# Eight padding copies made one per buffer, and expert blocks placed some steps earlier, in an attention and mixture-of-experts kernel

## The reference

```
qkv  = x @ qkv_w.T                       # q and k are rotated
attn = einsum(q, k) * SCALE + alibi
w    = softmax(attn);  out = w @ v       # per batch and head
x    = layernorm(x + out @ proj_w.T + proj_b)
shared = silu(x @ sW1 + sb1) @ sW2 + sb2
top_vals, top_idx = top_k(sqrt(softplus(x @ routing_W.T + bias)), 2)
y_e  = silu(x @ rW1[e] + rb1[e]) @ rW2[e] + rb2[e]      # e = 0..7
x    = layernorm(x + shared + sum over the two chosen e of top_val * y_e)
```

## Time and profile before

| | |
|---|---|
| median of three runs | 1526.68 us |
| profiled execution, its time | 1523.36 us |
| its span in the trace | 1521.5 us |
| PE busy | 1384.0 us, 91% |
| DVE busy | 1150.9 us, 76% |
| ACT busy | 1019.2 us, 67% |
| POOL busy | 722.4 us, 47% |
| moved by DMA | 242.07 MB, 159 GB/s on average |
| clock granted to TensorE, mean | 0.971 of full |

### The profile page before, as it was taken

How to read it: one execution, slowest core, us unless ns; L and a number is a source line. 1 busy time by engine, 2 the same in 40 slices (tenths; PEclk the granted TensorE clock), 3 DMA queues, 4 the chain that set the end, 5 groups by cost and what they waited for, 6 DMA issues and landing times.

```text
span 1521.5 us, 34124 instructions
## 1 busy us (share of the span) xinstructions
PE 1384.0 (91%) x11166; PEld 751.6 (49%) x11166; DVE 1150.9 (76%) x2632; ACT 1019.2 (67%) x1742; POOL 722.4 (47%) x654
## 2 busy tenths in 40 slices
PE   7889989999999989999999999999899988886777
PEld 4434444444444434555555544454455655445545
DVE  7777878788888887777776778778887777743677
ACT  1367767677777767777777777676677777765434
POOL 1434373645555454644526353625566443545441
PEclk8899999999999999999999999999999999999898
DMA  7434453434444334554656353445568777468542
GB/s 210 143 89 136 143 155 109 139 112 138 120 126 129 105 123 137 174 184 158 196 155 201 115 162 101 151 144 167 175 206 261 232 225 230 121 204 285 177 146 84
DMA packets 172777, 242.07 MB, mean 159 GB/s; under 512 B 58247, under 2 KB 91102, under 8 KB 172350
## 3 DMA queue, kind: packets, MB, share of 16 engines
q1 hardware_dynamic: 142170, 181.18, 39.3%
q0 software_dynamic: 10752, 29.37, 6.0%
q10 hardware_dynamic: 19684, 29.33, 5.5%
HBM read 152.53 MB, written 91.44 MB: 160 GB/s over the span
## 4 chain that ended last, share of the span: by engine, by line
PE 63%; DVE 13%; SPq 7%; issue 6%; DMA 5%; POOL 3%; ACT 3%; another core or an unknown queue 1%; ACTq 0%; POOLq 0%; DVEq 0%
PE pS L674 14%; PE pV L729 13%; PE pG L753 6%; PE pS L682 5%; DVE negm L990 4%; PE pG L762 4%; PE pG L775 3%; PE pG L856 3%; PE pG L864 3%; PE pG L848 2%; PE pG L837 2%; PE pT L706 1%; DMA rb<-d_rec 1%; ACT ee L1438 1%; PE pT L698 1%
## 5 line engine op out<-in xcount | busy, mean ns | idle before, releaser
L990 DVE TENSOR_REDUCE negm<-pS 128x1 f32<-128x512 f32 x1024 | 657.6, 682 | 210.5 <-PE pS L674 175.6
L1438 ACT ACTIVATE ee<-pT,slp 128x512 f32<-128x512 f32 x1024 | 650.9, 685 | 208.0 <-PE pT L698 171.4
L674 PE MATMUL pS<-ka,qa 62*128 62x512 f32 x1024 | 394.9, 453 | 7.4 <-ACT ee L1438 4.5
L698 PE MATMUL pT<-qa,ka 64*128 64x512 f32 x1024 | 393.4, 451 | 0.0
L682 PEld LDWEIGHTS pS<-mAB,tri 64*128 64x128 bf16 x2048 | 117.1, 96 | 424.2 <-issue 398.4
L682 PE MATMUL pS<-mAB,tri 64*128 64x64 bf16 x2048 | 236.9, 196 | 69.7 <-DVE negm L990 35.3
L729 PE MATMUL pV<-ee,vv 128*32 128x512 f32 (+1 forms) x2048 | 283.1, 625 | 0.0
L706 PE MATMUL pT<-mAB,tri 64*128 64x64 bf16 x2048 | 236.2, 196 | 4.5 <-ACT ee L1438 3.9
L1622 POOL TENSOR_TENSOR raw<-raw,rope 128x512 f32<-128x512 f32 x61 | 78.1, 1280 | 257.7 <-DVE sh L1027 257.1
L674 PEld LDWEIGHTS pS<-ka,qa 62*128 62x128 f32 x1024 | 172.6, 191 | 36.3 <-DVE negm L990 22.0
L698 PEld LDWEIGHTS pT<-qa,ka 64*128 64x128 f32 x1024 | 172.3, 190 | 0.0
(11 more groups left out here) (203 smaller groups left out, 2247.6 us busy)
## 6 DMA issues: line engine op xcount, KB each, us to landing
d_part<-parts SPq DMA_DIRECT2D x63, 512.0 KB, 2.8
qa<-d_part SPq DMA_DIRECT2D x378, 64.0 KB
wb<-in_wb SPq DMA_DIRECT2D x77, 256.5 KB
xg<-d_x SPq DMA_DIRECT2D x77, 256.0 KB
d_y<-yb ACTq DMA_DIRECT2D x77, 256.0 KB
ka<-d_part SPq DMA_DIRECT2D x128, 128.0 KB
xT<-in_xT SPq DMA_DIRECT2D x16, 512.0 KB
ka<-d_part SPq DMA_DIRECT2D x128, 64.0 KB
```

Source lines behind the costliest of these rows:

```text
L674: last = e.matmul(pS[:, k, :], qa[g % 4][r, i, t * 128:t * 128 + 128].bitcast(F32R), ka[g % 4][r, i, :].bitcast(F32R), start=(k == 1), sto ...
L698: last = e.matmul(pT[:, k, :], ka[g % 4][r, i, kt * 128:kt * 128 + 128].bitcast(F32R), qa[g % 4][r, i, :].bitcast(F32R), start=(k == 1), s ...
L990: e.tensor_reduce(negm[:, g % 2, j, t + k:t + k + 1], pS[:, k, :], AX, ALU.max, negate=True).then_inc(s_max, 1)
L1438: e.activation(ee[:, k, d % 7, :], pT[:, k, :], ACT.Exp, scale=slp[:, 6, h:h + 1]).then_inc(s_exp, 1)
```

## The change

Three things are changed. The paddings are issued as two DMAs, one for each buffer, at step 43, and each writes the 256 padding rows of all eight regions; before, two DMAs of one region each stood at the steps 43, 51, ... 99. The wait for them is for two DMAs' semaphore counts (32), where it was for sixteen (256). The blocks of the first group stand at 90 + 4j where they stood at 96 + 4j (the first 25 of them), and the first 27 blocks of the second group at 92 + 2j where they stood at 96 + int(1.85j). The later blocks of both groups, the third group and the final steps stay.

```
-BLOCKS_AT = ((96, 4.0, 25, 252, 4.0), (96, 1.85, 27, 148, 2.0), (104, 1.25, 15, 128, 3.0))
+BLOCKS_AT = ((90, 4.0, 25, 252, 4.0), (92, 2.0, 27, 148, 2.0), (104, 1.25, 15, 128, 3.0))
...
-                e.wait_ge(pad_w, 32 * E)
+                e.wait_ge(pad_w, 32)
...
-            if 0 <= s - PADS < 8 * E and (s - PADS) % 8 == 0:
-                r0 = (s - PADS) // 8 * REGION
+            if s == PADS:
                 for i in range(2):
-                    e.dma_start(d_x[i][r0:r0 + ROWS], A["x"][0, 0:ROWS]).then_inc(pad_w, 16)
+                    e.dma_start(d_x[i].rearrange("(x r) c -> r x c", x=E)[0:ROWS],
+                                A["x"][0, 0:ROWS].rearrange("r (x c) -> r x c", x=1).broadcast_to([ROWS, E, C])
+                                ).then_inc(pad_w, 16)
```

## The result

The changed kernel is slower: a median of 1540.94 us (1537.17 to 1551.62, six timed runs) against 1526.34 us for the kernel before on the same chip, a ratio of 1.0115 with a 95% interval of 1.0087 to 1.0143, that is +17.6 us (13 to 22). The two medians themselves differ by 14.6 us, and the median of all 25 runs of the changed kernel on record is 1543.1; I go by the ratio. I had forecast +7.7. The experiments ran on chips on which the kernel before took 1508.9, 1521.8, 1523.0 and 1527.1 us, so each is given by its ratio to the kernel before on its own chip, and in us as that ratio less one, times that median.

A forecast was written before the change was run, and what follows sets the result against it. PE was taken to bound the kernel, with 63% of the chain. Paddings +5.0, first group +3.7 and second group -1.0 made +7.7 us: 1531.1, given as 1534 us for a median run, range 1519 to 1543.

The forecast's parts named there:

- The burst: Two large copies at step 43 take 13.8 us of all sixteen engines, hold SP 11 us and delay step 48 by 8.5.
- +5.0 for the paddings: Copies at step 43: +8.5 us of delay at step 48, less 3.5 for the seven pairs of issues gone.
- The relief: Steps 48 to 112, small pairs gone from SP: three pairs worth up to 2.7 us, all seven 3.5, between 0 and 8.8.
- the 8.5 with SP held: Step 48: SP held behind the copies until about 126.5 us, so DVE's multiplication comes at 138.3, not 129.8; the delay taken.
- the 6.2 without: Step 48: SP not held, but its queue first in, first out; the reciprocals' rows land at 136, a delay of 6.2 us.
- What it gives back: Step 256, first group: DVE's 3.06 us wait for the reciprocals' rows shrinks as blocks move to remainders 7 and 3; -2.0 us.
- The standstill: Step 250: PE waits for the first block's rows, whose load waits for the last scatter; +5.7 us.
- The second group: 27 blocks spread over 52 steps, not 48, from step 444: no stall at the start; -1 us, between -8 and +5.
- the rival with -8: Burst absorbed, and the second group's even spacing worth half its idle time, -8 us; -7.8 in all, 1519 us; chance 0.15.
- absorbed: Step 48: engines take the copies beside other transfers, or operands have more slack; -0.8 us in all, 1526 us; chance 0.20.
- much slower: Step 48: 1 KB pieces from DRAM to DRAM go at half the rate; +21 us in all, 1548 us; chance 0.15.
- my case: Whole kernel: the main forecast, +7.7 us, 1534 us for a median run, running from 1528 to 1539; chance 0.50.

The follow-up runs named there:

- the pair at 94: Kernel before with the first group's blocks at 94 + 4j: loads at remainders 1 and 5, ratio 1.0011, +1.7 us; at 3 and 7, 1.0068, +10.4 us.

## Why the prediction was wrong

The sign was right, the size was not: +17.6 us for +7.7.

**The burst: right in kind, and its time came out partly by luck.** SP was held, but for less than my 11 us: the two issues behind the copies took 7.65 us, and the operands' issue ended at 130.4 us, where I had 132.6. Then the reciprocals took 3.8 us to land, where I had 2.15. The two errors offset each other, so that DVE's multiplication came at 137.84, near my 138.3 (in a kernel that was 1.0 us late at step 40). And it was the other wait that came first: I had PE waiting for the operands too, but less, and PE's 5.55 us of standstill are what made step 48 late. I said +5.0 for the paddings; from step 40 on they make 5.9 us at step 48, 7.9 at step 56 and 4.8 at step 144, and alone they time at +3.5 (-0.3 to +7.2). I left out the low clock, which may be part of the 1.9 us lost between the steps 48 and 56. The relief between the steps 80 and 144, which I had put at up to 2.7 us, comes out at about 1.5: the five traces without the pairs have 140.5 to 142.4 us there, 141.3 in the mean, and the ten that kept them in eight places from step 43 on 141.8 to 144.2, 142.8 in the mean. The kernel before, from which I took the 2.7, is one of the longest of these, 143.8.

The two things that I took from the Trainium skill, DMA: Bandwidth & Descriptors, are given there for DMAs that GpSimd issues, while the copies are SP's. No term of the sum rests on them. Of the two delays that the prediction weighed, the 8.5 with SP held and the 6.2 without, the trace shows that SP is held.

**The first group: the step that failed is "What it gives back", with the reason that blocks at the remainders 7 and 3 leave the pair of reciprocals alone.** I read the block's 3.1 us between the reciprocals out (L506) and the rows in (L516) as a delay. It is that once, at step 256, where DVE waited 3.06 us; that wait went down to 0.42 us as I said, and the eight steps from 256 are 1.6 us shorter. In the loads behind it, it is a cheap place: SP has to wait there anyway, until the reciprocals have landed. In the 13 groups of the steps 144 to 248, which have no loads of blocks, the kernel before waited there in nine, 11.3 us together; in the 11 groups from 264, with the loads in that place, once, for 0.5 us. Remainder 1, between the sums out and in, is such a place too. At remainders 3 and 7 the load's 3.1 us come on top, and the landings are waited for as well, 35.9 us in those 11 groups. SP was no longer ahead of the engines, and PE had to wait for its operands. The price of the new places was in my sum as nothing. My -2.0 was +9.6 by the run that moved only the loads, or +10.4 - 1.7 = +8.7 by the pair at 94. I had the number (SP's 129.5 us of waiting for DVE at L506) and took it for slack wherever a load stands; 20.1 us of it lay in these 88 steps, and the changed kernel has 2.2.

**The standstill: mis-sized.** 5.7 us were forecast at step 250; PE waited 3.94 us in the changed kernel, where a low clock had already made it late there, and 5.79 us in the run with the shift alone. My chain to it held: shifted by the 5.9 us by which the last scatter came late, it has the rows at 589.7, and PE went on at 589.45. But the price is not the wait. What 90 costs more than 94 is 18.3 - 10.4 = 7.9 us with the loads at 3 and 7, and 11.6 - 1.7 = 9.9 with them at 1 and 5; the intervals leave some 0 to 16 and 3 to 17. So the standstill is worth some 8 or 9, with these bounds; the 8.9 and 9.3 us by which the eight steps from 248 are longer, beyond their blocks' work, say the same. A part of the rest fits the clock: in the run with the shift alone it is at the lower level from 578.6 to 585.4 us, and PE goes on at 580.7. Some 4.7 us of work at half speed would lose up to 2.4 us, by my estimate, and 5.8 + 2.4 = 8.2. That was not tried apart.

**The second group:** -1 forecast, -1.4 measured (-5.3 to +2.7), not told from nothing, and the rival with -8 is out. **PE's order:** I gave it no term; the run at 94 with the loads at 1 and 5, +1.7 (-1.8 to +5.2), bounds it.

So +5.0 + 3.7 - 1.0 should have read about +3.5 + 18.3 - 1.4 = +20.4, which holds within the interval of the measured +17.6 (13 to 22). Of the rivals, absorbed and much slower are out by the trace at step 48. The way in which it went, my case with a second cost in the first group, I had not written down.

## What to carry to other kernels

On the engine that issues the DMAs in order, an issue had no price of its own here: it depended on the place. Behind a DMA whose landing the next instruction waits for, a load of 3.1 us filled that wait. Moved two steps from there, 25 loads cost 9.6 us of the whole: much less than the 78 us that they take on SP, since most of it still fell on waits. So look in the waits of that engine by line, before and after moving anything: when they turn from waits for the engines it serves into waits for its own landings, it has come to bound the stretch. Moving the blocks to an earlier step was worth nothing where a wait went with them, and a large transfer that nobody waits for delayed the small round trips behind it, in its own queue (3.8 us for a landing of 2.15) and from another (6.5 us).

## What the runs showed that I had not expected

With a standstill of PE of 3.9 to 5.8 us at step 48 or step 250 came 3.4 or 6.8 us at 1.2 GHz, in each of the six kernels that had one. The stretches of 6.8 us begin 1.5 to 2.1 us before PE goes on, so a part of them costs nothing. Even behind a wait of 1.7 to 1.9 us that PE has just ahead of step 248 in 13 of the traces, 3.4 us at 1.2 GHz stand in five of them. The trace of before has such stretches too, but none at these places.

An 8 KB DMA took 6.5 us to land beside 4.19 MB from another queue, three times its usual 2.15.

Stretches that an edit doesn't touch varied more between traces than I had thought: the 64 steps from 440 on took 223.2 to 232.4 us with the same list of blocks, and the 104 steps from 144 to 248, which no kernel changes, 227.8 to 235.1. A difference of two single traces of that size in a busy stretch says nothing by itself; I read -6.8 us there and timing gave -1.4.
